# A fused self-attention and correlation-grouped normalisation kernel: four tiles split into high and low parts instead of two, and score products on two halves of the array

## The reference, cut to what matters

```python
x_f = einsum('oc,bcn->bon', Wf, xf) + bf      # 16 x 1024 per image
x_g = einsum('oc,bcn->bon', Wg, xf) + bg      # 16 x 1024
x_h = einsum('oc,bcn->bon', Wh, xf) + bh      # 128 x 1024
s = einsum('bci,bcj->bij', x_f, x_g)          # 1024 x 1024 per image
beta = softmax(s, axis=-1)
x = x + gamma[0] * einsum('bci,bij->bcj', x_h, beta)
...
cos = einsum('bcn,bdn->cd', x_n, x_n) / B     # x_n: rows of x over their norms
_, idx = top_k(-abs(cos).T, 4)                # partners of each channel
# mean and variance over the four channels, then scale and shift
```

## Time and profile before

| | us |
|---|---|
| median of 3 runs | 214.97 (214.33 to 214.99) |
| span of the profiled execution, first to last instruction | 211.9 |
| PE busy | 186.4 (88%) |
| DVE busy | 173.7 (82%) |
| ACT busy | 143.9 (68%) |
| POOL busy | 34.3 (16%) |

### The profile page before, as it was taken

How to read it: one execution, slowest core, us unless ns; L and a number is a source line. 1 busy time by engine, 2 the same in 40 slices (tenths; PEclk the granted TensorE clock), 3 DMA queues, 4 the chain that set the end, 5 groups by cost and what they waited for, 6 DMA issues and landing times.

```text
span 211.9 us, 2596 instructions
## 1 busy us (share of the span) xinstructions
PE 186.4 (88%) x727; PEld 115.2 (54%) x727; DVE 173.7 (82%) x317; ACT 143.9 (68%) x256; POOL 34.3 (16%) x39
## 2 busy tenths in 40 slices
PE   7669979999999999999999999999999999983100
PEld 3435546465765676466756675657465756462000
DVE  6588989979898889979797979887988898766660
ACT  2548976799379955995499658984799378740320
POOL 0200210034003400160007100520034001001400
PEclk9999999999999999999999999999999999997555
DMA  6240002500060007000520052002200020000198
GB/s 207 89 162 0 0 0 100 203 0 0 39 257 3 0 0 292 6 0 3 205 94 0 0 186 111 0 0 99 99 0 0 3 99 0 0 0 0 53 403 336
DMA packets 4904, 16.16 MB, mean 76 GB/s; under 512 B 544, under 2 KB 672, under 8 KB 4896
## 3 DMA queue, kind: packets, MB, share of 16 engines
q1 hardware_dynamic: 4320, 14.68, 18.4%
q10 hardware_dynamic: 576, 1.38, 1.7%
HBM read 4.52 MB, written 4.19 MB: 41 GB/s over the span
## 4 chain that ended last, share of the span: by engine, by line
PE 71%; DVE 13%; ACT 6%; issue 5%; POOL 1%; DVEq 0%; ACTq 0%; POOLq 0%
PE o_ps L636 40%; PE s_ps L617 11%; PE w_ps L611 6%; PE w_ps L606 6%; DVE nmax L404 3%; PE w_ps L651 3%; ACT probs L318 3%; PE w_ps L645 2%; PE o_ps L603 2%; DVE y_all L596 1%; DVE probs_low L418 1%; DVE g_parts L427 1%; DVE y_cur L447 1%; ACT probs_high L324 1%; DVE values L435 1%
## 5 line engine op out<-in xcount | busy, mean ns | idle before, releaser
L318 ACT ACTIVATE probs<-s_ps,nmax 128x1024 f32<-128x1024 f32 x64 | 70.9, 1108 | 40.5 <-DVE nmax L404 40.5
L636 PE MATMUL o_ps<-probs,vnorm 128*128 128x512 f32 x192 | 90.2, 594 | 0.5 <-DVE y_cur L447 0.5
L404 DVE TENSOR_REDUCE nmax<-s_ps 128x1 f32<-128x1024 f32 x64 | 77.9, 1218 | 10.2 <-PE s_ps L617 9.8
L617 PE MATMUL s_ps<-g_parts,f_parts 128*128 128x512 f32 x128 | 51.6, 485 | 4.6 <-ACT probs L318 2.3
L636 PEld LDWEIGHTS o_ps<-probs,vnorm 128*128 128x128 f32 x192 | 35.3, 189 | 28.8 <-issue 23.2
L266 POOL TENSOR_TENSOR f_parts<-fg,fg_neg 64x512 fp32r<-64x512 f32 x14 | 24.0, 1713 | 122.1 <-ACT fg_neg L311 122.1
L617 PEld LDWEIGHTS s_ps<-g_parts,f_parts 128*128 128x128 f32 x128 | 21.2, 190 | 20.7 <-issue 14.0
L418 DVE TENSOR_TENSOR probs_low<-probs,probs_high 128x1024 fp32r<-128x1024 f32 x16 | 19.5, 1221 | 1.3 <-ACT probs_high L324 1.2
L427 DVE TENSOR_TENSOR g_parts<-fg,fg_neg 64x512 fp32r<-64x512 f32 x16 | 13.9, 871 | 6.6 <-ACT fg_neg L311 6.5
L335 ACT ACTIVATE vnorm<-values,rinv 128x128 f32<-128x128 f32 x48 | 18.8, 391 | 0.0
L611 PEld LDWEIGHTS w_ps<-wd,x_cur 128*128 128x128 f32 x112 | 14.7, 192 | 6.7 <-issue 6.7
(11 more groups left out here) (90 smaller groups left out, 165.7 us busy)
## 6 DMA issues: line engine op xcount, KB each, us to landing
x_all<-x_dram SPq DMA_DIRECT2D x7, 512.0 KB, 4.0
x_cur<-x_all SPq DMA_DIRECT2D x7, 512.0 KB, 3.2
y_all<-y_cur SPq DMA_DIRECT2D x7, 512.0 KB, 2.9
out_dram<-y_all SPq DMA_DIRECT2D x5, 512.0 KB, 5.8
out_dram<-y_all ACTq DMA_DIRECT2D x2, 512.0 KB, 4.1
x_all<-x_dram SPq DMA_DIRECT2D x2, 256.0 KB, 3.7
out_dram<-y_all SPq DMA_DIRECT2D x2, 256.0 KB, 2.2
wd<-wide_dram ACTq DMA_DIRECT2D x1, 256.0 KB, 4.3
```

What stands on the lines that cost most here:

```text
L318: nc.scalar.activation(probs[t][:, :], s_ps[t % 2][:, :], ACT.Exp, bias=nmax[:, t:t + 1], accum_out=rsum[:, t:t + 1]).then_inc(exp_done, 1)
L404: nc.vector.reduce_max(nmax[:, t:t + 1], s_ps[t % 2][:, :], AX_X, negate=True).then_inc(max_ready, 1)
L617: last = nc.tensor.matmul(s_ps[t % 2][:, h], f_parts[par][:, t * P:(t + 1) * P], g_parts[par][:, h], start=True, stop=True)
L636: last = nc.tensor.matmul(o_ps[:, halves[h]], weights[:, :], rows[:, halves[h]], start=(t == 0 and n == 0), stop=(t == T - 1 and n == len( ...
```

## The change

- **Split tiles.** `SPLIT` is now tiles 0, 2, 4 and 5. The probabilities of these tiles, not the values, are scaled by the inverse sums. For tiles 0 and 4 (`VECTOR_SPLIT`) ACT writes the scaled high part and DVE the low part; for 2 and 5 (`POOL_SPLIT`) POOL scales, copies and subtracts. The values of the four tiles are split once per image by POOL (`split_values`), unscaled.
- **Scores.** `fg_parts` holds f in rows 0 to 63 and g in rows 64 to 127; `gf_parts` holds them exchanged. The left half of the columns is multiplied over rows 0 to 63 of the array, the right half over rows 64 to 127.
- **Making the parts.** ACT writes `fg_neg` straight from PSUM, DVE adds it to the projection for all 128 rows (`parts`), and three transfers of SP per image exchange the halves (of image 0 DVE does it). The zeroed rows and `fg32` are gone.
- **Order.** `AHEAD` is 4. `project_fg` stands in steps 0 and 1, the transposes in 2 and 3, the values in 4 and 5, `gram` in step 6. `norm` (POOL) of the previous image stands behind `split_values`.
- **Gone.** `x_cur`, `y_cur` and `y_all` with their transfers: the result is written over `x_all`. The loops are written out for all stages.

```diff
-AHEAD = 3
-SCALED = 2
-SPLIT = (3, 7)
+AHEAD = 4
+VECTOR_SPLIT = (0, 4)
+POOL_SPLIT = (2, 5)
+SPLIT = (0, 2, 4, 5)
...
+            def split_probs(b, t):
+                n, count = SPLIT.index(t), pool_split_count(b, t)
+                pool.wait_ge(rinv_ready, T * b + t + 1)
+                nc.gpsimd.tensor_scalar(probs[t][:, :], probs[t][:, :], rinv[:, t:t + 1], 1.0,
+                                        ALU.mult, ALU.mult).then_inc(pool_scaled, 1)
+                pool.wait_ge(pool_scaled, count)
+                nc.gpsimd.tensor_copy(probs_high[n][:, :], probs[t][:, :]).then_inc(pool_high, 1)
+                pool.wait_ge(pool_high, count)
+                nc.gpsimd.tensor_tensor(probs_low[n][:, :], probs[t][:, :], probs_high[n][:, :].bitcast(F32),
+                                        ALU.subtract).then_inc(pool_low, 1)
...
+            for b in range(B):                       # ACT
+                for t in range(T):
+                    if b < L and t < H:
+                        negate_high(b + 1, t)
+                    nxt = ahead(b, t + AHEAD)
+                    if nxt[0] < B:
+                        exp(*nxt)
+                    nxt = ahead(b, t + AHEAD - 1)
+                    if nxt[0] < B:
+                        scale(*nxt)
+                    if b > 0 and t in (2, 3):
+                        high_yT(b - 1, t - 2)
+                    if b > 0 and t == 4:
+                        square(b - 1)
...
+            for b in range(B):                       # DVE
+                for t in range(T):
+                    if t == 0 and b >= 2:
+                        add_gram(b - 2, w_ps[:, BANK:BANK + P])
+                    if t < H and b < L:
+                        parts(b + 1, t)
+                    nxt = ahead(b, t + AHEAD)
+                    if nxt[0] < B:
+                        row_max(*nxt)
+                    nxt = ahead(b, t + AHEAD - 1)
+                    if nxt[0] < B:
+                        invert_sum(*nxt)
+                    if t == T - 1 and b >= 1:
+                        scale_gram(b - 1, w_ps)
+                    if t == T - 1:
+                        residual(b, 0)
+                        residual(b, 1)
+                    if nxt[0] < B and nxt[1] in VECTOR_SPLIT:
+                        low_part(*nxt)
+                    if b >= 1 and t in (3, 4):
+                        low_yT(b - 1, t - 3, w_ps[:, halves[t - 3]])
+                    if b < L and t in (5, 6):
+                        add_value_bias(b + 1, t - 5, w_ps)
...
-                for h in halves:
-                    last = nc.tensor.matmul(s_ps[t % 2][:, h], f_parts[par][:, t * P:(t + 1) * P],
-                                            g_parts[par][:, h], start=True, stop=True)
-                last.then_inc(scores, 1)
+                nc.tensor.matmul(s_ps[t % 2][:, halves[0]], fg_parts[b % 2][0:KP, tile],
+                                 gf_parts[b % 2][0:KP, halves[0]], start=True, stop=True)
+                nc.tensor.matmul(s_ps[t % 2][:, halves[1]], gf_parts[b % 2][KP:P, tile],
+                                 fg_parts[b % 2][KP:P, halves[1]], start=True, stop=True).then_inc(scores, 1)
```

More of the change, by code:

```diff
@@ L85, in build @@
         probs_low = [sb(f"probs_low{i}", [P, N], F32R) for i in range(len(SPLIT))]
-        v_high = [sb(f"v_high{i}", [P, P], F32R) for i in range(len(SPLIT))]
-        v_low = [sb(f"v_low{i}", [P, P], F32R) for i in range(len(SPLIT))]
         nmax = sb("nmax", [P, T])
@@ L365, in _, with scale @@
-            act.wait_ge(wfg_in, 16)
-            for h in range(H):
-                copy_fg(0, h)
-            for t in range(AHEAD):
-                exp(0, t, 0, fresh=True)
-                if t > 0:
-                    scale_values(0, t - 1, 0, fresh=True)
-            run_stages(act, stage)
-            def square(h):
+            def scale(b, t):
+                if t in POOL_SPLIT:
+                    return
+                act.wait_ge(rinv_ready, T * b + t + 1)
+                if t in VECTOR_SPLIT:
+                    nc.scalar.activation(probs_high[SPLIT.index(t)][:, :], probs[t][:, :], ACT.Copy,
+                                         scale=rinv[:, t:t + 1]).then_inc(high_ready, 1)
+                    return
+                act.wait_ge(v_ready, H * b + t // TH + 1)
+                nc.scalar.activation(vnorm[t][:, :], values[b % 2][:, t, :], ACT.Copy,
+                                     scale=rinv[:, t:t + 1]).then_inc(vn_ready, 1)
@@ L420, in split_parts @@
-                dve.wait_ge(vh_ready, split_count(b, t))
-                nc.vector.scalar_tensor_tensor(v_low[n][:, :], values[par][:, t, :], rinv[:, t:t + 1],
-                                               v_high[n][:, :].bitcast(F32), ALU.mult,
-                                               ALU.subtract).then_inc(vl_ready, 1)
-            def parts(to, rows, columns, done):
-                nc.vector.tensor_tensor(to[0:KP, columns], fg32[rows, columns], fg_neg[rows, columns].bitcast(F32),
-                                        ALU.add).then_inc(done, 1)
@@ L528, in _ @@
-            scale_gram(L - 1, w_ps)
-            for h in range(H):
-                dve.wait_ge(yT_high, L + 1 + h)
-                low_part(slice(h * TH, (h + 1) * TH), s_ps[h][:, halves[0]])
+            nc.vector.tensor_tensor(bias_neg[:, :], wd[:, BFG:BFG + 1], wd[:, NMASK:NMASK + 1],
+                                    ALU.mult).then_inc(bias_set, 1)
+            first_swapped(lower, upper, 0)
+            first_swapped(upper, lower, 0)
+            parts(0, 0)
+            parts(0, 1)
@@ new lines, in _ @@
+            row_max(0, 0)
+            first_swapped(upper, lower, 1)
+            dve.wait_ge(const_in, 16)
+            add_value_bias(0, 0, o_ps)
+            row_max(0, 1)
+            invert_sum(0, 0)
+            add_value_bias(0, 1, o_ps)
+            row_max(0, 2)
+            invert_sum(0, 1)
+            low_part(0, 0)
+            row_max(0, 3)
+            invert_sum(0, 2)
+            nc.vector.tensor_copy(ident_b[:, :], ident).then_inc(ident_ready, 1)
+            for b in range(B):
+                for t in range(T):
[20 more added lines that the diff above has]
+                        add_value_bias(b + 1, t - 5, w_ps)
@@ new lines, in attend @@
+            def attend(b, t):
+                if t in SPLIT:
+                    pe.wait_ge(vl_ready, H * b + t // TH + 1)
+                    if t in POOL_SPLIT:
+                        pe.wait_ge(pool_low, pool_split_count(b, t))
+                    else:
+                        pe.wait_ge(low_ready, vector_split_count(b, t))
+                    n = SPLIT.index(t)
+                    high, low = v_high[b % 2][:, t, :], v_low[b % 2][:, t, :]
+                    products = [(high, probs_high[n]), (low, probs_high[n]), (high, probs_low[n])]
@@ L624, in attend @@
                 else:
                     pe.wait_ge(vn_ready, whole_count(b, t))
+                    products = [(vnorm[t][:, :], probs[t])]
                 for h in range(H):
[L627 to L634 removed]
+                    if t == 0 and b > 0:
+                        pe.wait_ge(y_ready, H * (b - 1) + h + 1)
```

501 lines of the change are left out of this document (220 added, 281 removed).

## The result

The changed kernel takes 271.69 us (median of 4 runs, 271.16 to 272.05). The kernel before took 214.8 us in the same comparison. The ratio is 1.265, with a 95% interval from 1.2627 to 1.2672. The forecast was 257.0 us in a range of 246 to 272: the sign and the mechanism came as forecast, the size fell short by 14.7 us, and the measured time lies only 0.3 us inside the upper end of the range.

What follows compares the result with a forecast made beforehand. PE bounds the kernel, DVE right behind; the new queue order makes a 27.4 us loop per stage. 211.9 + 2 + 5.7 + 6 x 5.15 + 2 = 252.5 us span, 3.1 around it: 255.6; POOL +1.5: 257 us, range 246 to 272.

Steps and rivals of the forecast that it cites:

- The rival in which PE stays the bound: Waits don't form in the stages; PE's 19.7 to 21.6 us per stage decide: 195, or about 210 us; chance 0.04.
- POOL as the bound: POOL's 1024-column operations take 3.4 us each, tiles 2 and 5 come late: period 31.5, 293 us; over 275: chance 0.08.
- The +1.5 us: Allowance for POOL's one-input operations on 1024 columns, between no cost at 1.2 us each and 6 us in all at 2.4.
- the +2 for that stage: Last stage, with no parts and one low part: 2 us more.
- The forecast's own case: The stage's loop through the engines sets the time: period 27 to 28 us, 255 to 259 us; chance 0.45.
- the eight links: The loop of one stage, summed link by link over PE, ACT, DVE and POOL: 27.4 us against 22.24.
- the link with attends 0 and 1: Start of the stage's loop: attend 0, scores at 0.24, attend 1, projection and its result: 4.4 us.
- The link with the projection in front of the turned gram: End of the stage's loop: gram_high and gram_rows, the way to PE, projection, turned gram: 1.8 us.
- POOL's link: In the stage's loop: copy and subtraction of 256 columns 1.15, nsq 0.3, rnorm 0.6: 2.05 us.
- its 5.7: First stage: the same two waits of DVE and ACT without the gram link, 5.7 us more.
- the change of array shape costs: Rival: 0.17 us lost at each of 16 shape changes a stage, two to four in the loop: 260 to 263; chance 0.25.
- the halves do not overlap: Rival: a score pair's halves run one behind the other, 0.46 us a pair, 0.3 a stage: 259 us; chance 0.1.

Runs made afterwards that it cites:

- both moves: Changed kernel with DVE's low part one step later, and ACT's negation and DVE's parts behind their step's exponential and row maximum: 240.71 us.
- the filled waits: Changed kernel with six products of zeros added behind tiles 2 and 3 of every stage, in PE's waits: 264.31 us.
- the reordered kernels: Changed kernel with five moves in the queues and no work changed: 226.04 us with score products on halves, 223.22 us on all 128 rows.
- all rows: Changed kernel with the score products alone put back on all 128 rows, g alone copied across and zeros in the other rows: 268.22 us.
- both on the same rows: Kernel before, with both score products of a pair on rows 0 to 63: 236.03 us, against 223.47 us with halves at once.

## Why the prediction was right, and by how much not

**Right, with its cause.** PE lost the bound to a loop through DVE, ACT, POOL and PE, made by the order of the queues: moving steps in the queues alone brought 271.7 down to 226.0. The rival in which PE stays the bound (195 or 210) was far off. POOL as the bound (293) did not come either: its operations on 1024 columns took 1.12, 1.04 and 2.38 us, 4.5 us for a tile where 4.8 to 7.2 were feared. The +1.5 us that I took for it was not needed in the six stages, where PE waits at most 0.3 us for a low part, off the chain. In the last stage it waits 2.43 us for one, and that wait is on the chain; the +2 for that stage had other reasons and came out at 2.1, which is luck. In all the six stages POOL came to the front (9.3 us of waits) only once both moves had been made. The exchange stayed hidden (2.2 us to landing). POOL and DVE did not collide (low parts on DVE are 1.28 us throughout).

**The range held in part by luck.** 271.69 us is at the edge of a range whose upper part stood for late POOL operations and for the change of shape. The forecast's own case was 255 to 259 with a stage of 27 to 28 us, and neither came. What lifted the time to the edge was the clock, held at full speed by the prediction (7.0 us), and links that were a little longer than summed (6.3 us).

**Mis-sized: the sum by 16.8 us of span, in three terms.**

- *The clock, 7 us.* The sum was made at the full clock throughout, since the stage of the earlier trace rows had 1.00 in it. But that row belongs to a PE without gaps, and the forecast itself gave PE waits of 2 us at two places of each stage. That was the step to doubt. Filling the waits gave 7.0 us of span back: 1.1 up to the first residual and 6.0 in the six stages.
- *The links, 1.1 us a stage, 6.3 in six.* Six of the eight links were longer. In the link with attends 0 and 1, the score pair was put at 0.24 and took 0.42 with 0.1 more behind it. The link with the projection in front of the turned gram took 0.3 us more: behind a wait that projection is 1.10 long, and 0.87 otherwise. POOL's link took 0.24 more: 1.30 for the copy and subtraction of 256 columns in place of 1.15, and 0.69 for `rnorm` with the step to DVE in place of 0.6. The low part on DVE is 1.28 long and not 1.22, the negation 0.79 and not 0.73. A link worked out to the nearest 0.1 from rows of slightly different instructions comes out short, and here six of eight were short.
- *The start and first stage, 2.9 us beside the clock.* The first attend began 3.1 us later, not 2 (16.53 before, 19.62 after), and the first stage lost 1.8 us more than its 5.7. In it is what the first fall of the clock costs, from 12 to 23 us, which the filled waits left in place; it was not measured apart.

The three make 16.2 us; the other 0.6 lie in the last stage and behind it. The span fell short by 16.8; the +1.5 for POOL and 0.7 us less around the span than I had taken make it 14.7.

**The array.** The sum took the pair as 0.23 us cheaper; it is 0.14 dearer, where PE is the bound. PE's own work was put at 19.7 us a stage with halves at once and at 21.6 with full-height pairs. In the reordered kernels it measured 22.98 and 22.07. The first is 3.3 us off, and the pair is most of it; where the 0.5 us of the second come from no run shows. That error did not move the forecast much, because PE isn't the bound of the changed kernel: there all rows and halves differ by 0.2 us in a clean stage. The rival "the change of array shape costs" had the right mechanism and nearly the right price: 0.17 at each of 16 changes of shape in a stage, where the traces show 0.2. Its sign came too: neighbours of score pairs stand 0.33 to 0.43 us apart. It was right beside the main case and not in place of it. The rival "the halves do not overlap" is refuted: both on the same rows is 12.6 us slower.

**Not settled.** Whether longer runs of 64-row products would pay no run shows: every pair here stands between 128-row products. Nor is it known what decides whether the clock falls after the same idle time. And the 2.9 us of the start have no link of their own.

## What to carry to other kernels

Write down for each in-order queue what stands behind an instruction that will wait, and sum the loop link by link: busy times fell on PE's helpers here while one instruction placed one step too early cost 32 of 57 us, some 7 of them by the clock. When a forecast gives the matmul engine waits that it did not have, work out the case of the lower clock too: here it was 1.5 us in four of six stages. Packing two half-height products pays only against the switch into and out of their shape: here it took 0.4 us for each pair and gave back 0.2. Pairs that stand together would share one switch, by estimate; that was not tried.

## What the runs showed of the hardware

- Two 64-row products of 512 columns on different halves start within 0.01 us of each other and end as one; among 128-row products the pair cost 0.14 us more than two full products (0.34 more if they share rows). A change between 128-row and 64-row products costs 0.2 us in either direction, half before the first product of the new shape and half behind it.
- Products of zeros on an idle TensorE made the kernel 7.4 us faster: with its waits filled, no slice between the start and the tail had a granted clock below 0.9, where it fell five times in that stretch without them.
- GpSimd took 1.12 us for a scaling and 1.04 for a cast of 1024 columns, and 2.38 for a subtraction of two operands, about twice as long as with one; on 256 columns the cast took 0.40 and the subtraction 0.73.
